# Attention of batches 1 and 2: MLP in 256-row halves, its second product on row halves of TensorE between two attention steps

## What is computed

```python
def _L0_attn_ref(x, w_in, b_in, w_out, b_out, w1, b1, w2, b2, ln1_g, ln1_b, ln2_g, ln2_b):
    xn = _ln(x, ln1_g, ln1_b)
    q, k, v = split(xn @ w_in.T + b_in, 3)            # 16 heads of 16
    scores = q k^T / 4, masked: (idx % 8 == 0)[:, None] | eye
    x = x + softmax(scores) v @ w_out.T + b_out
    xn = _ln(x, ln2_g, ln2_b)
    return x + gelu(xn @ w1.T + b1) @ w2.T + b2       # MLP of width 1024, blocks "M"

def _L0_ffn_ref(hidden, gate_W, gate_b, wi_W, wi_b, wo_W, wo_b, lora_A, lora_B):
    expert = argmax(softmax(hidden @ gate_W.T + gate_b))         # of 8
    inter = relu(hidden @ wi_W.T + wi_b + lora of that expert)   # width 1024, blocks "F"
    return inter @ wo_W.T + wo_b

x = layernorm(x + attn(x)); x = layernorm(x + ffn(x))
```

## Time and profile before

| | |
|---|---|
| profiled execution, first to last instruction (its own time) | 1437.3 us |
| runs | 1438.65, 1441.14, 1442.77 us |
| TensorE (PE) busy | 1386.3 us, 96% |
| weight loads (PEld) busy | 1066.3 us, 74% |
| VectorE (DVE), ScalarE (ACT), GpSimd (POOL) busy | 59%, 51%, 45% |
| mean granted TensorE clock | 0.995 of 2.4 GHz |
| first scores to last weighted sum of batch 1 | 480 to 655 us |
| the same of batch 2 | 823.5 to 998.5 us |

### The profile page before, as it was taken

The page is one execution under the profiler, slowest core; times in us unless marked ns, Lnnn a source line. Parts: engine busy times, 40 slices in busy tenths (PEclk is TensorE's granted clock), DMA queues, the critical chain, the costliest instruction groups (busy, mean ns, idle before and its releaser), DMA issues.

```text
span 1437.3 us, 26412 instructions
## 1 busy us (share of the span) xinstructions
PE 1386.3 (96%) x10103; PEld 1066.3 (74%) x10103; DVE 854.4 (59%) x1823; ACT 734.6 (51%) x1103; POOL 647.8 (45%) x533
## 2 busy tenths in 40 slices
PE   6799999999999999999999999999999999999997
PEld 5688665678888766668888866667888876556996
DVE  6748576636656666555647576763675657762332
ACT  3444555553544555564444555555444455655442
POOL 3554321328754414145865432333776442132755
PEclk9899999999999999999999999999999999999999
DMA  7565223215561132212682213220556212310100
GB/s 246 161 181 107 57 45 67 55 38 192 190 164 47 50 68 51 56 45 84 210 214 62 74 38 75 57 53 20 189 189 158 74 45 44 80 26 23 52 16 30
DMA packets 91394, 130.51 MB, mean 91 GB/s; under 512 B 8314, under 2 KB 68180, under 8 KB 88148
## 3 DMA queue, kind: packets, MB, share of 16 engines
q1 hardware_dynamic: 91268, 128.82, 32.9%
HBM read 68.08 MB, written 60.57 MB: 90 GB/s over the span
## 4 chain that ended last, share of the span: by engine, by line
PE 79%; DVE 10%; POOL 4%; issue 2%; ACT 2%; DMA 0%; SPq 0%; POOLq 0%; DVEq 0%; ACTq 0%
PE ps L1567 19%; PE ps L1568 16%; PE ps L1569 16%; PE ps L1756 8%; PE ps L1745 7%; PE ps L1730 4%; DVE mx L1442 3%; PE ps L1803 2%; PE ps L1791 2%; PE ps L1825 2%; DVE stats L1316 2%; POOL rows L1042 1%; ACT prob L1172 1%; PE ps L1688 1%; PE ps L1762 1%
## 5 line engine op out<-in xcount | busy, mean ns | idle before, releaser
L1442 DVE TENSOR_REDUCE mx<-ps 128x2 f32<-128x1024 f32 x256 | 311.1, 1223 | 179.0 <-PE ps L1730 176.9
L1172 ACT ACTIVATE prob<-ps 128x1024 f32<-128x1024 f32 x256 | 262.6, 1026 | 180.4 <-PE ps L1745 180.2
L1057 POOL TENSOR_TENSOR hid1l<-gel,hid1h 128x512 fp32r<-128x512 f32 x85 | 111.2, 1309 | 202.2 <-ACT hid1h L1214 202.1
L1057 POOL TENSOR_TENSOR hid2l<-gel,hid2h 128x512 fp32r<-128x512 f32 x85 | 111.1, 1307 | 197.6 <-ACT hid2h L1214 197.5
L1057 POOL TENSOR_TENSOR hid0l<-gel,hid0h 128x512 fp32r<-128x512 f32 x86 | 112.4, 1307 | 191.6 <-ACT hid0h L1214 191.5
L1206 ACT ACTIVATE gel<-ps,cols 128x512 f32<-128x512 f32 x128 | 88.2, 689 | 180.7 <-PE ps L1569 169.5
L1745 PEld LDWEIGHTS ps<-qslot,kslot 50*128 50x128 f32 x1024 | 76.2, 184 | 91.0 <-issue 65.8
L1208 ACT ACTIVATE gel<-ps 128x512 f32<-128x512 f32 x128 | 76.6, 598 | 120.9 <-PE ps L1825 119.7
L1756 PE MATMUL ps<-prob,vals 128*32 128x256 f32 x2048 | 137.5, 385 | 0.2
L1745 PE MATMUL ps<-qslot,kslot 50*128 50x256 f32 x1024 | 128.9, 330 | 4.2 <-ACT prob L1172 4.1
L1730 PE MATMUL ps<-kslot,qslot 48*128 48x512 f32 x512 | 105.8, 424 | 4.8 <-DVE mx L1442 4.4
(11 more groups left out here) (245 smaller groups left out, 3943.9 us busy)
## 6 DMA issues: line engine op xcount, KB each, us to landing
k_d<-kst SPq DMA_DIRECT2D x192, 128.0 KB
kslot<-k_d SPq DMA_DIRECT2D x64, 384.0 KB
xin<-in_L_attn_x SPq DMA_DIRECT2D x32, 256.0 KB, 4.3
rows<-xs_d SPq DMA_DIRECT2D x16, 512.0 KB, 6.3
y_d<-rows SPq DMA_DIRECT2D x15, 512.0 KB, 3.1
rows<-y_d SPq DMA_DIRECT2D x15, 512.0 KB, 4.5
out<-rows SPq DMA_DIRECT2D x15, 512.0 KB, 3.2
xs_d<-xin SPq DMA_DIRECT2D x28, 256.0 KB, 2.7
```

The source lines that it names most:

```text
L1057: nc.gpsimd.tensor_tensor(hid[i % RING][1][:], gel[i % 2][:], hid[i % RING][0][:], ALU.subtract).then_inc(lo_done, 1)
L1172: nc.scalar.activation(prob[(n - 1) % 2][:].rearrange("p e i q -> p (e i q)"), ps[:, 0:2, :].rearrange("p a n -> p (a n)"), ACT.Exp).then_ ...
L1442: nc.vector.tensor_reduce(best[:, :, j % NQ], ps[:, at:at + 2, :], AX.X, ALU.max).then_inc(maxr_done, 1)
```

## The change

For the attention of batches 1 and 2 (`NARROW`) a second function writes the order, and the three F blocks beside it are computed otherwise:

- "up" (i, k) now takes all of 256 contraction rows for two hidden tiles, but only 256 of the block's rows: 6 matmuls of 256 columns where there were 3 of 512; the last one of L1825 becomes two of 256. Items 0 to 3 of a block make its rows 0 to 255, items 4 to 7 its rows 256 to 511.
- "dn" (i, h) contracts over 64 partitions at a time: each of its 6 matmuls becomes two, one on each row half of the array, into banks 6 and 7. Both banks hold a part of the same sum, so "sum" comes twice in a block and adds both banks, one after the other.
- dn (i, 0) and dn (i, 1) stand together with a step ahead of them and one behind. Where a third step is due it stands between up 0 and up 1.
- The short work uses bank 2 (mt, ot) or 3 (tn, ga, pi), which mx also uses, in place of bank 5. It stands behind up 1.
- The activation is a step of its own ("gl"), in narrow blocks behind the short work. No Gelu block runs there, so that branch is not used.
- The last two "at" of the batch go into the first item after it.

```diff
+NARROW = [what == "attention" and 0 < b < B - 1 for what, b in PHASE]
+    def attention_narrow(b):
+        def step():
+            s = taken[0]
+            taken[0] += 1
+            if s % 2 == 0:
+                weighted(s - 2)
+                weighted(s - 1)
+            put(("sc", b, s // KK, s % KK))
+            maxima(s)
+            turns(s)
+            moves(s)
+            while late:
+                put(late.pop(0))
+        middle = [0] + [FT * q + f for q in range(len(blocks)) for f in (range(2, 6) if q + 1 < len(blocks) else range(2, FT))]
+        for j in range(n):
+            put(("up", i, 0))
+            if j in middle:
+                step()
+            put(("up", i, 1))
+            pending.append(i)
+            hook = {0: [("tn", ready, 0)], 1: [("tn", ready, 1), ("xw", ready)], 3: [("ga", ready)], 7: [("pi", ready)]}.get(f, [])
+            for one in hook:
+                put(one)
+            if alone:
+                for one in alone.pop(0):
+                    put(one)
+            put(("gl", i))
+            put(("ev", i))
+            step()
+            down(0)
+            down(1)
+            step()
-        _banks = [UP if _beside else OUT]
+        _banks = [OUT if not _beside else UP if not _small else MX if _w in ("mt", "ot") else MX + 1]
+    elif _w == "dn" and NARROW[_s[1] // FT]:
+        _banks = [DOWN, DOWN + 1] if _s[1] % HF == 0 and _s[2] == 0 else []
+                    if NARROW[k]:
+                        dve.wait_ge(down_done, FT * k + HF * (h + 1))
+                        for e in range(2):
+                            if e:
+                                dve.wait_ge(sum_done, SUM_AT[(k, h)] - 1)
+                            nc.vector.tensor_tensor(part, part, ps[:, DOWN + e, :], ALU.add).then_inc(sum_done, 1)
+                        for m in range(KT):
+                            last = three(ps[:, UP, AW * k:AW * k + AW], [t[:, m, P * tile:P * tile + P] for t in wup[w]],
+                                         [t[:, m, rest] for t in turned[blk % 2]], k == 0 and m == 0, w == "M" and m == KT - 1)
+                        for j in range(2):
+                            at = AW * h + P * j
+                            for r, (one, w) in enumerate(((0, high), (0, low), (1, high))):
+                                for e in range(2):
+                                    half = slice(HALF * e, HALF * e + HALF)
+                                    last = mm(ps[:, DOWN + e, D * j:D * j + D], hid[i % RING][one][half, at:at + P], w[half, tile, :],
```

More of the change, by code:

```diff
@@ L23 @@
 FT = F // P
+HF = FT // 2
 NQ = NT // STRIDE
@@ L94, in down, with close @@
             pending.pop(0)
[L95 to L104, removed]
+            close(i)
+    def close(i):
+        if NARROW[i // FT]:
+            if i % HF == HF - 1:
+                put(("sum", i // FT, i % FT // HF))
+        elif i % FT == FT - 1:
+            for h in range(2):
+                put(("sum", i // FT, h))
     def piece(b, q, part):
@@ L160, in rows_in @@
             put(("ld", k + 2))
-    mine = [0]
+    mine, carry = [0], []
     def mx(b):
@@ L468 @@
         FINAL[_s[1:]] = AT * (len(FINAL) + 1)
+SUM_AT = {}
+for _s in STEPS:
+    if _s[0] == "sum":
+        SUM_AT[_s[1:]] = max(SUM_AT.values(), default=0) + (2 if NARROW[_s[1]] else 1)
 IN, MX, OUT, UP, DOWN, KQ = 3, 2, 4, 5, 6, 2
@@ L1817, in step @@
                         pe.wait_ge(d_setup, lows(BIAS_AT - 1))
+                    if NARROW[blk]:
+                        if f == 0 and k == 0:
+                            pe.wait_ge(turnl_done, N("tn", blk, 1))
+                        rest = slice(AW * (f // HF), AW * (f // HF) + AW)
+                        tile = 2 * (f % HF) + k
+                        for m in range(KT):
+                            last = three(ps[:, UP, AW * k:AW * k + AW], [t[:, m, P * tile:P * tile + P] for t in wup[w]],
+                                         [t[:, m, rest] for t in turned[blk % 2]], k == 0 and m == 0, w == "M" and m == KT - 1)
+                        if w == "F" and k == 1:
+                            if f == 0:
+                                pe.wait_ge(ust_done, N("pi", blk))
+                            for g in range(2):
+                                tile = 2 * (f % HF) + g
+                                last = mm(ps[:, UP, AW * g:AW * g + AW], bst[:, P * tile:P * tile + P], ust[:, rest],
+                                          start=False, stop=True, skip_group_check=True)
+                        if k == 1:
+                            last.then_inc(up_done, 1)
+                        return
                     if f == 0:
@@ L1831, in step @@
                     pe.wait_ge(lo_done, i + 1)
+                    if NARROW[blk]:
+                        tile = 2 * (f % HF) + h
+                        high, low = wdn[BLOCKS[blk][0]]
+                        for j in range(2):
[4 more added lines that the diff above has]
+                                    last = mm(ps[:, DOWN + e, D * j:D * j + D], hid[i % RING][one][half, at:at + P], w[half, tile, :],
+                                              start=f % HF == 0 and h == 0 and j == 0 and r == 0,
+                                              stop=f % HF == HF - 1 and h == 1 and r == 2, skip_group_check=True)
+                        last.then_inc(half_done if h == 0 else down_done, 1)
+                        return
                     for j in range(2):
```

91 lines of the change are left out of this document (78 added, 13 removed).

## The result

The changed kernel takes 1445.4 us (median; 1441.9 to 1447.1) where the kernel before takes 1440.3 in the same comparison: a ratio of 1.0035, interval 1.0023 to 1.0047. That is 5.1 us slower. The forecast was 1441, "within 0.3%". The time lies in the predicted range, but the loss is just over the bound of 4.3 us, so the forecast of no change was wrong.

What follows compares the result with a forecast made beforehand. TensorE, full of matmuls and shape changes, was taken to bound both attentions. Per batch, -7.5 shape changes +0.8 projection +11.9 new waits -5 old ones gave +0.2 us, +0.4 for both: forecast 1441 us, range 1429 to 1455.

Steps and rivals of the forecast that it cites:

- the bound of 4.3 us: Whole kernel: 0.3%, the smallest difference from no change that a measurement of it can tell.
- What bounds the kernel: Attention of batches 1 and 2: TensorE sets the time, busy 172.8 of 175.0 us, full of matmuls and shape changes.
- The rival that the change does not do what it says: Gaps between matmuls come from change of work, not tile shape, so dn saves nothing between steps: 1456 us, chance 0.04.
- halves in turn: Rival for dn: its row halves run one after the other, 33.7 us more a batch, 1508 us; chance 0.03.
- Shape changes, -7.5 us: Attention of one batch: tile-shape changes fall from 159 to 122, saving 7.5 us.
- +0.8 in the projection: Next projection: two items' dn end up there and bring four new shape changes of 0.2, 0.8 us back.
- Matmuls, put at 0: up, LoRA and dn in the attentions: the new matmuls cost the same as the old ones, no difference.
- Waits, 11.9 for 5 that go: Attention of one batch: new waits, mostly for the maximum, add 11.9 us in place of 5 us of old ones.
- mx behind tn: Six places where mx waits for VectorE's subtraction, 0.25 us each, 1.5 us a batch.
- the late maxima: LayerNorm, picks or a sum ahead of a maximum on VectorE: ten places of 0.1 to 0.5, one of 1.3, 3.5 us.
- a point of decision of 13.8 us: Waits in a batch's attention above which the changed kernel would be measurably slower.
- The rival that VectorE falls behind altogether: Late maxima stop transposes, which stop the next mx: 18.6 us of waits a batch, 1455 us; chance 0.21.

Runs made afterwards that it cites:

- E3: Changed kernel's order and banks, but up of 512 columns and dn as whole matmuls, as before the change: 1453.1 us, ratio 1.0082.
- E1: Changed kernel with VectorE's maximum taken over 64 of 512 columns, the other 448 left out: 1419.5 us, ratio 0.9858.
- E2: Kernel before the change with the maximum taken over 64 of 512 columns, the other 448 left out: 1425.9 us, ratio 0.9893.
- E7: Changed kernel with one addition in place of two at the end of each half block, bank 7's part left out: 1442.5 us, ratio 1.0010.
- E4: Changed kernel with each maximum taken as two instructions, one per bank, each with its own signal: 1459.1 us, ratio 1.0127.
- E9: Changed kernel with both additions behind the next step's maximum and pt moved to the batch's last output, nothing left out: 1440.9 us, ratio 1.0006.
- E10: As E9, and also LayerNorm's pieces and the picks of experts put behind a maximum, the second pick one step later: 1451.2 us, ratio 1.0073.
- E6: Changed kernel with short work and some third steps moved away from a maximum just begun, pt no longer right behind pi: 1446.5 us, ratio 1.0045.
- E8: Changed kernel with the short work back in bank 5, behind the activation, as before the change: 1484.5 us, ratio 1.0308.

## Why the prediction was wrong

- **What bounds the kernel.** Right. The gaps between matmuls belonged to the shape, not to the change of work: with the shape kept there is none (mx to dn 0.23), and E3 brings them back. The rival that the change does not do what it says is out, as is the one of halves in turn (0.119 a pair, not 0.234). The Trainium skill's rule that a load goes by columns, whatever the rows (TensorE: Matmul & The Clock Gate, section LDWEIGHTS (loading the stationary operand)), which speaks against halving them, did not decide here: a pair with its two loads costs 0.119, a whole one with its load 0.118.
- **Shape changes, -7.5 us, and +0.8 in the projection.** Right in size: E1 against E2 gives -6.4 us by the medians and -7.1 by the traces, where the budget with these two has -6.6.
- **Matmuls, put at 0. The first step that failed.** "A pair costs 0.12 in sc, and a whole one 0.117 to 0.12: the same." They are nearly the same, and so are two matmuls of 256 columns and one of 512, but not quite: 0.1193 for a pair against 0.1184, and 0.1177 for 256 columns against 0.2322 for 512. These are 11 ns in a dn, 19 in an up and 6 in the LoRA matmul, and with 24 items in a batch 0.9 us a batch, 1.7 us in all. The prediction rounded to hundredths and then multiplied by some 600 matmuls.
- **Waits, 11.9 for 5 that go. The second step that failed.** 12.7 came for 4.5 that went: +8.2 where +6.9 was taken. The kinds were right (the short work, mx behind tn, the late maxima, exp), and their sizes within 1.2 us, too high for the short work (0.345 each; the exposed load was counted on top, but the wait already holds it) and for the late maxima, too low for exp and for mx, which waited at 17 places and not 14. That their sum came out near is in part luck, since these misses cancel. What was missing is pt behind pi, 0.85 us: pi used the bank that pt uses, and the list of new waits went by banks 2 and 3 as the maxima use them, not by every pair of uses of bank 3.
- Together 0.9 for the pace, 0.85 for the new waits and 0.5 for the old ones that stayed are 2.2 us a batch, 4.5 in all: nearly the whole error. Both are terms mis-sized by little; the forecast lay on the edge between "same" and "slower", and a point of decision of 13.8 us of waits is passed by 12.7 with 0.9 of pace and the 0.5 of old waits that stayed.
- **VectorE.** "They cost only where a maximum queued behind them is due" was right, and E7 measures it: 1.5 to 2 us a batch of the 4.1 that the additions last. The rival that VectorE falls behind altogether did not come; E4, where 0.07 us more on each maximum brings longer waits for it, shows how little room is left.
- **Sentence for sentence.** "Pairs at 0.12 with no gap": seen. "Issue waits down by about a quarter": a third, 32.1 to 21.4 us. "Waits for the maximum at nine and more places": 15. "mx waiting for tn's subtraction six times": five, 0.12 to 0.23 us each. "Waits over 14 would show it wrong": they did not get there.

What stays open: why the clock falls in one execution and not in another behind a wait of the same length (E7 and the changed kernel), and why the stretches behind E9's attentions grew.

## What to carry to other kernels

When work is put where a shape change vanishes, list for every bank that is shared afterwards each pair of uses that follow one another, and put whatever the reading engine does besides behind the instruction that frees the bank: in E9 two moves gave back 4.5 of 5 us that way. What is moved must be done before that instruction's next turn (E10). A wait that is only moved to another place comes back at the next step if the chain of steps is as long as before (E6), so first ask which instruction sets the distance from step to step; here it is the maximum, and with it short the same change wins 6.4 us (E1, E2). And do not round a pace that is multiplied by hundreds: 1.5 ns on each of some 600 matmuls was 0.9 us.

## What the runs showed of the hardware

- Two matmuls of 256 columns on the two row halves follow the two before them at 0.119 us, one of 128 rows the one before it at 0.118 (means over batch 1). Before, this could be read only from sc with its four loads at once.
- A maximum over 2 x 512 columns takes 1.22 us, one over 512 columns 0.685: two of the latter take 0.07 us more from start to end than one of the former, and over 2 x 64 columns it still takes 0.29.
- The granted clock, which was 1.00 in the attentions of both kernels, fell to its lower level of 1.2 GHz in five other runs (E3, E4, E7, E8, E10), behind a wait and while TensorE was busy again. In E4:

```profile
527.30 0.50 PE L1855 MATMUL ps<-kslot,qslot 48*128 48x512 f32 x2 [1.44 <-DVE mx L1558]
...
530.50 0.41 PE L1693 MATMUL ps<-turned0h,wil 128*128 128x256 f32 x1
530.72 0.41 PE L1691 MATMUL ps<-turned0h,wih 128*128 128x256 f32 x1
```

  The matmuls of up come at 0.21 us from 528.6 to 535.4. In E10 it was a wait of 1.53 us (above). The length of the wait alone does not decide it: E3 falls (0.83 at 520 to 530) behind a wait of 0.72 us and E7 (0.84 at 870 to 880) behind one of 0.92, while the changed kernel waits 0.91 us at that place in each batch, and no stretch of ten microseconds in its attentions is under 1.00. What else decides it, no run here shows. Where it came, a fall cost between 1.6 us (E7) and 5 us (E10) on TensorE, which no sum of waits holds.
